# A gated long convolution with adapters: in the last stage's rounds, the projection ahead of the turn of the next gated tile

## The chip, the cores and the metric

The kernel runs on one core of a Trainium2 chip. The metric is device time of one execution in microseconds (us). Engines are TensorE (PE in the rows, PEld its weight loads), VectorE (DVE), ScalarE (ACT), GpSimd (POOL) and SyncE (SP, which issues most of the loads).

## What is computed

The input x is 8 sequences of 2048 rows with 512 channels, all float32. Two residual layers follow one another. The first is a Hyena layer, the second a weighted sum of 8 of 32 adapters, which is one 512 x 512 matrix and one bias for all rows.

```python
x = x + hyena(layernorm(x))
x = x + ffn(layernorm(x))

# hyena
proj = (x @ in_proj_w + in_proj_b).reshape(B, L, C, 3)
v = conv3(proj[..., 0]) + short_b
for i in range(2):
    conv = irfft(rfft(v) * rfft(coefs[:, :, i]))[:, :L]   # long convolution
    output = proj[..., i + 1] * conv
return output @ out_w + out_b

# ffn
return einsum('k,kod,bsd->bso', weights, W[ids], x) + einsum('k,ko->o', weights, b[ids])
```

Only the last branch reaches the output, so one long convolution and one gate are computed.

## The kernel before

The kernel has four parts: `prep` makes the filters' spectrum, `front` the normalised input, its two projections and the first transform, `middle` the product with the filter in the frequency domain, and `back` everything behind. The change is in `back`.

`back` works on 128 tiles of 128 rows and 512 channels, 16 for each of the 8 sequences. For each tile t:

- conv (L1361): the last step of the inverse transform, on TensorE, into the bank b_psC. Four matmul instructions with 64 columns of weights for each tile; `conv_pair` does two tiles in every second round.
- gate: GpSimd makes the correction at the sequence's edges (`correct`, L1294 and L1296, one product and one subtraction), VectorE adds it to b_psC (L1435) and multiplies with the gate from memory into b_o (L1440, the semaphore o_done).
- turn_o (L1375): four TensorE transposes of b_o into the bank b_psP, which is a single one (semaphore p_ps).
- o_high on ScalarE (L1312) copies b_psP, rounded to the matmul's type, into b_oh; o_low on VectorE (L1452) takes the rest into b_ol (o_lo). With it b_psP is free again.
- project: twelve matmuls of 512 columns (L181 to L183), high by high, high by low and low by high over four blocks of channels, into b_psO (o_ps).
- residual on VectorE: the sum with x (L1460, y_done), bn_stats (L1462), bn_aggr (L1468, mv_done). GpSimd makes scale and shift of it (`scalars`, L1276 to L1281, norm_ready) and then the sum of y and the second bias (`bias_y`, L1302). ScalarE's norm (L1318, z_done) writes the normalised tile b_z.
- turn_z (L1392), z_high (L1325), z_low (L1472): the same turn and split for b_z, through the bank b_psT.
- adapt: twelve matmuls into b_psF (L181 to L183, ff_ps). VectorE's finish (L1479) adds b_yb, and ScalarE's queue issues the store.

Each engine runs its own in-order program, and semaphores tie them together. The helper `pipelined` writes each engine's program: in round s it calls every stage in the list's order, with tile s minus the stage's lag. The same list stands for the first rounds (fill), the loop over the sequences and the last rounds (drain). The order inside a round is thus that of the list alone. VectorE's list is gates of tile s-1, residual s-3, z_low s-4, o_low s-1, finish s-5, bias_x s (L1429). ScalarE's is z_high s-4, o_high s-1, norm s-3, store s-6. GpSimd's is correct s, scalars s-3, bias_y s-3. SyncE loads the convolved rows (b_fin, waits for c_ps), the gate (b_gin, waits for o_done) and x (b_xin, waits for y_done).

On TensorE an odd round s does conv of tiles s-1 and s, turn_z of s-4, adapt of s-5, turn_o of s-1 and project of s-2. An even round does adapt of s-5, turn_z of s-4, turn_o of s-1 and project of s-2. The two forms of turn_z are why a pair of rounds repeats and not one.

Of the kernel before, what the change touches and what calls it, by code (L numbers as in the profile page):

```python
# [14 lines left out]
B = 8  # L15
# [6 lines left out]
T = 16  # L22
# [112 lines left out]
def pipelined(eng, outer, tiles, stages):  # L135

    fill = max(lag for _, lag in stages)

    def step(i, s, last):
        for stage, lag in stages:  # L140
            t = s - lag
            if t >= tiles and not last:
                stage(i + 1, t - tiles)
            elif 0 <= t < tiles:
                stage(i, t)

    for s in range(fill):
        step(0, s, False)

    def one_pass(i, last):  # L150
        for s in range(fill, tiles + fill):
            step(i, s, last)

    one_pass(0, False)
    with eng.Fori(1, outer - 1) as i:
        one_pass(i, False)
    one_pass(outer - 1, True)


def old(b, t, n):  # L160

    return not (isinstance(b, int) and b * T + t < n)


def hyena_adapter_kernel(nc, x, in_w, in_b, short_w, short_b, fw1, fb1, fw2, fb2, fw3, fb3,
# [13 lines left out]
    def mm3(pe, out_ps, w_hi, w_lo, d_hi, d_lo, first, last):  # L179

        pe.matmul(out_ps, w_hi, d_hi, start=first, stop=False)  # L181
        pe.matmul(out_ps, w_hi, d_lo, start=False, stop=False)  # L182
        return pe.matmul(out_ps, w_lo, d_hi, start=False, stop=last)  # L183
# [949 lines left out]
    def back(bc, kept):  # L1133
        with ExitStack() as st:
# [64 lines left out]
            def no(b, t):  # L1199
                return b * T + t  # L1200

            def early(b, t):
                return isinstance(b, int) and b == 0 and t < EARLY
# [7 lines left out]
            def turned_at(b, t):  # L1211
                if isinstance(b, int) and b == 0 and t in TURN_AT:
                    return range(2 * TURN_AT.index(t), 2 * TURN_AT.index(t) + 2)
                return ()
# [126 lines left out]
            @block.tensor  # L1341
            def _(pe):
                pe.wait_ge(kept["s4_in"], 16)
                pe.wait_ge(bc["ident_in"], 16)

                def turn_w(b, t):
                    for d in turned_at(b, t):
                        if d >= 2:
                            pe.wait_ge(wf_lo, d - 1)
                        for ot in range(CT):  # L1350
                            mm = pe.transpose(psF[d % 2][:, ot * P:(ot + 1) * P], res[:, ot, d * P:(d + 1) * P], ident[:])
                        mm.then_inc(wf_ps, 1)

                def conv(b, t):
                    pe.wait_ge(f_in[t % 2], 16 * (b * (T // 2) + t // 2 + 1))
                    if early(b, t):
                        pe.wait_ge(bc["tail_in"][t], 48)
                    if old(b, t, 2):
                        pe.wait_ge(a_done, no(b, t) - 1)
                    for h in range(2):  # L1360
                        mm = pe.matmul(psC[t % 2][h * N1:(h + 1) * N1, :], s4[:, h * T + t, :], fin[:, t % 2, h, :], start=True, stop=True)  # L1361
                    mm.then_inc(c_ps, 1)

                def conv_pair(b, t):

                    if t % 2:
                        conv(b, t - 1)
                        conv(b, t)

                def turn_o(b, t):  # L1370
                    pe.wait_ge(o_done, no(b, t) + 1)
                    if old(b, t, 1):
                        pe.wait_ge(o_lo, no(b, t))
                    for ct in range(CT):
                        mm = pe.transpose(psP[:, ct * P:(ct + 1) * P], o[:, t % 2, ct * P:(ct + 1) * P], ident[:])  # L1375
                    mm.then_inc(p_ps, 1)

                def project(b, t):
                    pe.wait_ge(o_lo, no(b, t) + 1)
                    if old(b, t, 2):  # L1380
                        pe.wait_ge(y_done, no(b, t) - 1)
                    for ct in range(CT):
                        mm = mm3(pe, psO[t % 2][:], oh[:, t % 2, ct * P:(ct + 1) * P], ol[:, t % 2, ct * P:(ct + 1) * P],
                                 woh[:, ct], wol[:, ct], ct == 0, ct == CT - 1)
                    mm.then_inc(o_ps, 1)

                def turn_z(b, t):
                    pe.wait_ge(z_done, no(b, t) + 1)
                    if old(b, t, 1):
                        pe.wait_ge(z_lo, no(b, t))  # L1390
                    for ct in range(CT):
                        mm = pe.transpose(psT[:, ct * P:(ct + 1) * P], z[:, t % 2, ct * P:(ct + 1) * P], ident[:])  # L1392
                    mm.then_inc(t_ps, 1)

                def turn_z_behind_conv(b, t):
                    if t % 2:
                        turn_z(b, t)

                def turn_z_behind_adapt(b, t):
                    if t % 2 == 0:
                        turn_z(b, t)

                def adapt(b, t):
                    pe.wait_ge(z_lo, no(b, t) + 1)
                    if isinstance(b, int) and b * T + t == 0:
                        pe.wait_ge(wf_lo, CT)
                    if old(b, t, 2):
                        pe.wait_ge(res_done, no(b, t) - 1)  # L1410
                    for ct in range(CT):
                        mm = mm3(pe, psF[t % 2][:], zh[:, t % 2, ct * P:(ct + 1) * P], zl[:, t % 2, ct * P:(ct + 1) * P],
                                 wfh[:, ct], wfl[:, ct], ct == 0, ct == CT - 1)
                    mm.then_inc(ff_ps, 1)

                pipelined(pe, B, T, [(conv_pair, 0), (turn_w, 0), (turn_z_behind_conv, 4), (adapt, 5), (turn_z_behind_adapt, 4), (turn_o, 1), (project, 2)])

            @block.vector
            def _(dve):
# [150 lines left out]
```

## Time and profile before

| | us |
|---|---|
| median of 3 runs | 2336.48 (2334.76 to 2341.91) |
| the profiled execution | 2337.87 |
| its span, first to last instruction | 2336.1 |
| TensorE busy | 2292.4, 98% |
| VectorE busy | 1530.6, 66% |
| GpSimd busy | 933.2, 40% |
| ScalarE busy | 855.8, 37% |

Busy time is a union over the whole span. The matmuls' ends are modelled and neighbours overlap, so distances are best taken from start to start. A bracket behind a timeline row says how long the engine was idle ahead of it and what released it. Bytes moved are 493.98 MB, at a mean of 211 GB/s.

### The profile page before, as it was taken

What the parts mean: (1) busy time and instruction counts of PE and PEld (TensorE: products, weight loads), DVE (VectorE), ACT (ScalarE), POOL (GpSimd) and SP (SyncE); (2) the same over time, 40 slices, a digit from 0 to 9 for tenths busy, and PEclk for the clock granted to TensorE, in tenths of its full rate; (3) what the DMA queues carried; (4) which work ended last, traced back from release to release, by engine and by line L of the source; (5) the groups of instructions that cost most, each with busy time, mean ns of one, the idle gap of its engine ahead of it and who ended that gap; (6) DMA issues with size and microseconds to landing.
All of it is one profiled execution on the core that took longest, in us unless ns stands there. A gap on an engine that the chain in (4) does not pass through costs nothing.

```text
span 2336.1 us, 39721 instructions
## 1 busy us (share of the span) xinstructions
PE 2292.4 (98%) x12804; PEld 1588.9 (68%) x12804; DVE 1530.6 (66%) x2180; ACT 855.8 (37%) x1155; POOL 933.2 (40%) x1183
## 2 busy tenths in 40 slices
PE   8899999999999999999999979999999999999999
PEld 2577777777777777543343337777777777777777
DVE  7644434444444434467777767888888888888886
ACT  5444444444444444344444432222222222222222
POOL 2222222222222222000000027777777777777775
PEclk9999999999999999999999989999999999999999
DMA  8645454545454456588999988765666666666663
GB/s 293 209 164 184 144 167 144 180 166 191 137 184 159 150 182 242 221 331 358 370 359 359 359 308 259 213 180 177 180 180 180 177 178 177 177 180 178 177 179 105
DMA packets 179725, 493.98 MB, mean 211 GB/s; under 512 B 19139, under 2 KB 19460, under 8 KB 158796
## 3 DMA queue, kind: packets, MB, share of 16 engines
q1 hardware_dynamic: 149964, 392.47, 51.2%
q10 hardware_dynamic: 29696, 100.68, 12.2%
q8 instruction: 35, 0.57, 0.1%
q14 instruction: 30, 0.25, 0.0%
HBM read 274.93 MB, written 218.12 MB: 211 GB/s over the span
## 4 chain that ended last, share of the span: by engine, by line
PE 54%; DMA 3%; SPq 0%; POOL 0%; issue 0%; DVE 0%; ACT 0%; DVEq 0%; POOLq 0%
PE m_psW L1046 8%; PE m_psA L1029 7%; PE b_psF L183 5%; PE b_psF L181 5%; PE b_psF L182 5%; PE b_psC L1361 5%; PE b_psO L181 5%; PE b_psO L183 5%; PE b_psO L182 5%; PE b_psT L1392 3%; PE b_psP L1375 2%; DMA m_xin<-spec 1%; DMA b_fin<-wide_out 0%; DMA b_fin<-spec 0%; DMA spec<-wide_out 0%
## 5 line engine op out<-in xcount | busy, mean ns | idle before, releaser
L1129 DVE TENSOR_TENSOR m_m<-m_psA,m_spec 128x1024 f32<-128x1024 f32 x256 | 301.3, 1219 | 103.9 <-PE m_psA L1029 86.3
L764 POOL TENSOR_TENSOR vl<-v,vh 128x512 fp32r<-128x512 f32 x128 | 165.2, 1291 | 389.7 <-ACT vh L722 389.7
L1046 PE MATMUL m_psW<-m_m,mats 64*64 64x512 f32 x2048 | 250.1, 592 | 2.0 <-issue 1.7
L1325 ACT ACTIVATE b_zh<-b_psT 128x512 fp32r<-128x512 f32 x128 | 76.5, 598 | 460.5 <-PE b_psT L1392 460.5
L865 DVE TENSOR_TENSOR gto<-psG,bgr 128x512 f32<-128x512 f32 x128 | 87.5, 683 | 195.2 <-PE psG L183 195.1
L181 PE MATMUL psV<-wvh,nth 128*128 128x512 f32 x512 | 213.3, 417 | 0.6 <-DVE ntl L846 0.6
L181 PE MATMUL b_psO<-woh,b_oh 128*128 128x512 f32 x512 | 211.2, 413 | 0.0
L1029 PE MATMUL m_psA<-m_xin,mats 64*64 64x512 f32 x1536 | 201.6, 598 | 6.4 <-PEq L555 3.0
L722 ACT ACTIVATE vh<-v 128x512 fp32r<-128x512 f32 x128 | 80.9, 632 | 340.6 <-DVE v L858 340.6
L181 PE MATMUL b_psF<-wfh,b_zh 128*128 128x512 f32 x512 | 205.4, 401 | 0.0
L182 PE MATMUL psV<-wvl,nth 128*128 128x512 f32 x512 | 200.6, 392 | 0.0
L183 PE MATMUL psV<-wvh,ntl 128*128 128x512 f32 x512 | 200.4, 391 | 0.0
L183 PE MATMUL b_psF<-wfh,b_zl 128*128 128x512 f32 x512 | 200.2, 391 | 0.0
L183 PE MATMUL b_psO<-woh,b_ol 128*128 128x512 f32 x512 | 200.1, 391 | 0.0
L182 PE MATMUL b_psO<-wol,b_oh 128*128 128x512 f32 x512 | 199.7, 390 | 0.0
L183 PE MATMUL psG<-wgh,ntl 128*128 128x512 f32 x512 | 199.5, 390 | 0.0
L181 PE MATMUL psG<-wgh,nth 128*128 128x512 f32 x512 | 199.2, 389 | 0.0
L182 PE MATMUL psG<-wgl,nth 128*128 128x512 f32 x512 | 199.2, 389 | 0.0
L182 PE MATMUL b_psF<-wfl,b_zh 128*128 128x512 f32 x512 | 199.1, 389 | 0.0
L846 DVE TENSOR_TENSOR ntl<-psT,nth 128x512 fp32r<-128x512 f32 x128 | 88.1, 688 | 168.4 <-ACT nth L716 168.4
L1085 ACT ACTIVATE wide_out<-m_psW 128x1024 f32<-128x1024 f32 x128 | 131.1, 1024 | 171.7 <-PE m_psW L1046 171.7
L1046 PEld LDWEIGHTS m_psW<-m_m,mats 64*64 64x64 f32 x2048 | 94.4, 133 | 129.7 <-issue 128.9
(138 smaller groups left out, 4652.4 us busy)
## 6 DMA issues: line engine op xcount, KB each, us to landing
spec<-wide_out SPq DMA_DIRECT2D x64, 1024.0 KB, 9.0
spec<-wide_out ACTq DMA_DIRECT2D x64, 1024.0 KB, 6.5
b_fin<-spec SPq DMA_DIRECT2D x126, 512.0 KB, 4.6
m_xin<-spec SPq DMA_DIRECT2D x30, 2048.0 KB, 10.0
xg<-in_L_attn_x_dram SPq DMA_DIRECT2D x64, 512.0 KB, 6.2
gate_d<-gto SPq DMA_DIRECT2D x32, 1024.0 KB, 4.0
b_gin<-gate_d SPq DMA_DIRECT2D x128, 256.0 KB, 3.6
b_xin<-in_L_attn_x_dram SPq DMA_DIRECT2D x256, 128.0 KB, 3.2
```

What stands on the lines that cost most here:

```text
L181: pe.matmul(out_ps, w_hi, d_hi, start=first, stop=False)
L182: pe.matmul(out_ps, w_hi, d_lo, start=False, stop=False)
L183: return pe.matmul(out_ps, w_lo, d_hi, start=False, stop=last)
L722: act.activation(vh[:, t % 2], v[:, t % 2], ACT.Copy).then_inc(v_hi, 1)
L764: pool.tensor_tensor(vl[:, t % 2], v[:, t % 2], vh[:, t % 2].bitcast(F32), ALU.subtract).then_inc(v_lo, 1)
L846: dve.tensor_tensor(ntl[:, t % 2], psT[t % 2][:].rearrange("p (k r) -> p k r", k=CT), nth[:, t % 2].bitcast(F32), ALU.subtract).then_inc(n ...
L865: dve.tensor_tensor(gto[:, slot, t % SUB], psG[:], bgr[:], ALU.add).then_inc(g_out, 1)
L1029: mm = pe.matmul(psA[k % RA][half[q], slot, :], w[half[slot]], xin[half[slot], par, B if k < 2 else 2 * (k - 2) + q, :], start=True, stop= ...
L1046: mm = pe.matmul(psW[pair % 2][half[slot], q, :], ws[slot][half[q]], m[half[q], pair % RM, part, slot, :], start=part == 0, stop=part == 1)
L1085: act.activation(wo[:, par, 2 * pair:2 * pair + 2, :], psW[pair % 2][:], ACT.Copy).then_inc(w_out, 1)
L1129: dve.tensor_tensor(m[:, (k - 2) % RM, part], psA[k % RA][:], spec[:, par, part], ALU.mult).then_inc(m_done, 1)
L1361: mm = pe.matmul(psC[t % 2][h * N1:(h + 1) * N1, :], s4[:, h * T + t, :], fin[:, t % 2, h, :], start=True, stop=True)
```

## The change

In TensorE's list of stages for `back`, `project` (lag 2) now stands ahead of `turn_o` (lag 1). A round thus ends with the turn of the tile gated in it, and the next round begins behind that. The instructions are the same in kind and number, each has the same waits and semaphores, and the other engines' programs are untouched.

```diff
--- before.py
+++ after.py
@@ -1413,7 +1413,7 @@
                                  wfh[:, ct], wfl[:, ct], ct == 0, ct == CT - 1)
                     mm.then_inc(ff_ps, 1)
 
-                pipelined(pe, B, T, [(conv_pair, 0), (turn_w, 0), (turn_z_behind_conv, 4), (adapt, 5), (turn_z_behind_adapt, 4), (turn_o, 1), (project, 2)])
+                pipelined(pe, B, T, [(conv_pair, 0), (turn_w, 0), (turn_z_behind_conv, 4), (adapt, 5), (turn_z_behind_adapt, 4), (project, 2), (turn_o, 1)])
 
             @block.vector
             def _(dve):
```

## Rows read from the trace of the kernel before

**Rows 1.** Busy time by stretch: from:to, length, each engine's busy us, clock, DMA.

```profile
1310.00:1410.00 100.00, 87.06 (x663) 41.80 (x656) 68.87 (x76) 37.34 (x43) 23.99 (x30) 0.93 0.87 318
1510.00:1610.00 100.00, 100.00 (x492) 74.99 (x490) 84.06 (x124) 26.49 (x41) 73.97 (x97) 1.00 0.62 180
```

**Rows 2.** Timeline of TensorE, one pair of rounds: start us, duration us, instruction.

```profile
1741.09 1.94 PE L1361 MATMUL b_psC<-b_fin,b_s 128*64 128x512 f32 x8
...
1742.95 0.66 PE L1392 MATMUL b_psT<-b_ident,b_z 128*128 128x128 f32 x4
...
1743.37 0.47 PE L181 MATMUL b_psF<-wfh,b_zh 128*128 128x512 f32 x1
...
1746.20 0.60 PE L1375 MATMUL b_psP<-b_ident,b_o 128*128 128x128 f32 x4
...
1746.55 0.47 PE L181 MATMUL b_psO<-woh,b_oh 128*128 128x512 f32 x1
...
1749.38 0.39 PE L181 MATMUL b_psF<-wfh,b_zh 128*128 128x512 f32 x1
...
1752.11 0.60 PE L1392 MATMUL b_psT<-b_ident,b_z 128*128 128x128 f32 x4
...
1752.54 0.60 PE L1375 MATMUL b_psP<-b_ident,b_o 128*128 128x128 f32 x4
...
1752.90 0.48 PE L181 MATMUL b_psO<-woh,b_oh 128*128 128x512 f32 x1
...
1755.81 1.94 PE L1361 MATMUL b_psC<-b_fin,b_s 128*64 128x512 f32 x8
```

**Rows 3.** Timeline of ScalarE, behind the first turn_o of rows 2.

```profile
1746.83 0.60 ACT L1312 ACTIVATE b_oh<-b_psP 128x512 fp32r<-128x512 f32 x1 [2.59 <-PE b_psP L1375]
```

**Rows 4.** Timeline of all engines, from one bn_aggr through o_low to the next.

```profile
1789.92 0.18 DVE L1468 BATCH_NORM_AGGREGATE b_mv<-b_stats 128x2 f32<-128x6 f32 x1 [0.18 <-DVE b_stats L1462]
...
1790.99 0.60 ACT L1312 ACTIVATE b_oh<-b_psP 128x512 fp32r<-128x512 f32 x1 [2.59 <-PE b_psP L1375]
...
1791.36 1.30 POOL L1302 TENSOR_TENSOR b_yb<-b_y,adb_sum 128x512 f32<-128x512 f32 x1
...
1791.62 0.69 DVE L1452 TENSOR_TENSOR b_ol<-b_psP,b_oh 128x512 fp32r<-128x512 f32 x1 [0.95 <-ACT b_oh L1312]
...
1792.63 1.28 POOL L1294 TENSOR_TENSOR b_corr<-b_edge_b,b_v 128x512 f32<-128x512 f32 x1
1792.83 1.63 DVE L1429 TENSOR_TENSOR b_xin<-b_xin,bor 128x512 f32<-128x512 f32 x1
...
1793.99 1.62 POOL L1296 TENSOR_TENSOR b_corr<-b_edge_b,b_corr 128x512 f32<-128x512 f32 x1
...
1797.67 0.18 DVE L1468 BATCH_NORM_AGGREGATE b_mv<-b_stats 128x2 f32<-128x6 f32 x1 [0.18 <-DVE b_stats L1462]
```

**Rows 5.** Timeline, bn_aggr and the norm that waited for it through GpSimd.

```profile
1782.09 0.18 DVE L1468 BATCH_NORM_AGGREGATE b_mv<-b_stats 128x2 f32<-128x6 f32 x1 [0.18 <-DVE b_stats L1462]
...
1783.61 0.82 ACT L1318 ACTIVATE b_z<-b_y,b_shift,b_rstd 128x512 f32<-128x512 f32 x1 [0.34 <-POOL b_shift L1281]
```

**Rows 6.** Timeline of the fill, norm and a turn_z that waited for it.

```profile
1403.02 0.81 ACT L1318 ACTIVATE b_z<-b_y,b_shift,b_rstd 128x512 f32<-128x512 f32 x1 [3.40 <-POOL b_shift L1281]
...
1403.89 0.66 PE L1392 MATMUL b_psT<-b_ident,b_z 128*128 128x128 f32 x4 [0.42 <-ACT b_z L1318]
```

**Rows 7.** Timeline of VectorE near the end, first and last of eight instructions.

```profile
2306.82 0.69 DVE L1452 TENSOR_TENSOR b_ol<-b_psP,b_oh 128x512 fp32r<-128x512 f32 x1 [1.47 <-ACT b_oh L1312]
...
2311.55 0.18 DVE L1468 BATCH_NORM_AGGREGATE b_mv<-b_stats 128x2 f32<-128x6 f32 x1 [0.18 <-DVE b_stats L1462]
```

**Rows 8.** Groups by line: busy us, mean ns of one | idle us before them.

```profile
L1429 DVE TENSOR_TENSOR b_xin<-b_xin,bor 128x512 f32<-128x512 f32 x128 | 145.8, 1139 | 7.4 <-DMA b_xin<-in_L_attn_x_dram 4.2 <-PEq L884 3.2
...
L1440 DVE TENSOR_TENSOR b_o<-b_corr,b_gin 128x512 f32<-128x512 f32 x128 | 141.4, 1105 | 13.3 <-DVE b_corr L1435 10.0
```

**Rows 9.** DMA issues on the page: count, KB each, median us to landing.

```profile
b_fin<-spec SPq DMA_DIRECT2D x126, 512.0 KB, 4.6
```

## Prediction

> **What bounds the kernel now.** I read the page's slices first, then stretches of the last stage. From 1.41 ms to the end TensorE is at 100% with the full clock, while VectorE stands at 84%, GpSimd at 74% and ScalarE at 26% [rows 1]. The last stage is a repeating pair of rounds: an odd round A (conv_pair, turn_z, adapt, turn_o, project) and an even round B (adapt, turn_z, turn_o, project). TensorE's timeline gives it without a hole: A from 1741.09 to 1749.38, B to 1755.81, a pair of 14.72 us, 7.36 a tile [rows 2]. Starting with round 5 there are 61 such periods. So time can only come from shorter work on TensorE or go into waits that TensorE doesn't have now. VectorE is next: its own queue has little over one microsecond to spare in a round, and it is chained to TensorE through ScalarE.
>
> **What is moved on TensorE.** Nothing is added or taken away: four transposes of turn_o(s-1) go behind the twelve matmuls of project(s-2). Its waits go with it: turn_o waits for o_done(s-1) and o_lo(s-2), project for o_lo(s-2) and y_done(s-4). All four are met earlier today than either needs them, so project can move up at no cost.
>
> Junctions first. An adapt or project behind its own kind takes 2.73 us (B's adapt), behind a transpose 2.83 (A's adapt and project), and 2.91 where the conv follows it; a turn takes 0.35 to 0.36 ahead of a project, 0.43 where another turn follows, and 0.42 behind the conv; the conv takes 1.86 [rows 2]. After the change A is 1.86 + 0.42 + 2.83 + 2.73 + 0.35 = 8.19, and B is 2.83 + 0.35 + 2.83 + turn_o. A turn followed by the conv isn't in the trace; its bounds are 0.35 and 0.43, and I take 0.40, as a change of kind of work cost 0.08 on the other side. B is 6.41, the pair 14.60. Without any wait the change would save 0.12 a pair, 61 x 0.12 = 7.3 us.
>
> **What the move delays.** turn_o now starts 2.7 us later in its round, and everything that hangs on it does too: o_high on ScalarE, o_low on VectorE. Behind o_low in VectorE's queue stand finish, bias_x, and the next round's gate (two operations), residual (add, bn_stats, bn_aggr) and z_low. Behind o_high in ScalarE's queue stands norm. TensorE doesn't need o_low soon, there is an adapt between. But it needs norm, and norm needs bn_aggr, which stands in VectorE's queue behind the o_low of the round before. That closes a loop through all engines. From the turn_o that ends round A:
>
> - turn_o to o_high: 1746.20 to 1746.83, 0.63 [rows 2, 3]
> - o_high to o_low: 1790.99 to 1791.62, 0.63 [rows 4]
> - o_low to the bn_aggr of round B: X, eight VectorE instructions, below
> - bn_aggr through four small GpSimd steps to norm: 1782.09 to 1783.61, 1.52 [rows 5]
> - norm to turn_z, where TensorE did wait for it once: 1403.02 to 1403.89, 0.87 [rows 6]
> - turn_z of the next round A 0.42, adapt 2.83, project 2.73, and then turn_o again [rows 2]
>
> The loop is 9.63 + X and runs once in a pair. If it is over 14.60, that is X over 4.97, TensorE waits at turn_z of round A; against today's 14.72 the change loses from X = 5.09 on. Today turn_o of A stands ahead of project, so the same loop is 2.73 shorter, 6.90 + X, and never binds.
>
> **The size of X.** Undisturbed it is 4.73 (2306.82 to 2311.55, near the kernel's end) [rows 7]. Two of the eight read two SBUF operands, bias_x and the gate's product; undisturbed they take about 0.68, but on average 1.139 and 1.105 [rows 8], so 0.46 + 0.42 more, which gives X = 5.61. One of the longest is 1791.62 to 1797.67, 6.05 [rows 4]. The same rows show why: bias_x issued at 1792.83 ends 0.55 after the GpSimd product of 1792.63 (1.28 long), so it waited for that instruction to end, and the GpSimd subtraction issued at 1793.99 took 1.62 in place of 1.28, behind bias_x. Either engine waits out the other's instruction.
>
> The Trainium skill says so too (SBUF — State Buffer, "SBUF: two separate sides"): VectorE with two SBUF inputs and GpSimd take their shared ports by an exclusive lock, and the loser blocks for the whole instruction. By these rows the trace agrees. A reader who takes the lock for a mere sharing would use the mean of 5.61; one who goes by the rule has to ask which instruction meets which, and the next paragraph does so from rows.
>
> After bn_aggr of round A GpSimd starts bias_y 1.44 later, the product 2.71 and the subtraction 4.07 later, the last until about 5.35 [rows 4]. In the new steady state o_low of A starts 9.63 - Y after that same bn_aggr, Y being VectorE's way from B's bn_aggr to A's: 4.73 and one z_low (some 0.7) and its own waits of about 0.9 to 1.0, so 6.4. Then o_low stands at 3.2 and bias_x, 1.21 behind it [rows 4], at 4.4: inside the subtraction, till 5.35 + 0.55. It takes some 1.4 in place of 0.6, and the gate's product then meets no GpSimd work. That gives X = 5.55. Both ways agree; I take 5.6. Bounds: 4.73 and 6.05.
>
> **Sum.** Pair: 9.63 + 5.6 = 15.23, against 14.72: +0.51, of which TensorE's wait is 0.63 and the junctions give 0.12 back. 61 x 0.51 = 31 us. The profiled execution has a time of 2337.9 (span 2336.1), 1.4 over the median of 2336.5; 2337.9 + 31 = 2369. The fill and the last rounds have other bounds and I cost them at nothing: the fill waits for transfers, and in the drain the last project stands behind an adapt either way.
>
> **What else is moved past, at no cost.** TensorE issues no DMAs. SP's loads follow c_ps, o_done and y_done. The gate's product and residual come up to 2.7 us later in the round; the load of the convolved rows behind them takes 4.6 us to land [rows 9] and is needed at the next conv_pair, a pair of over 14 us later. If that cover were gone, a conv would be late by what is missing, but some 4 us are left. finish comes later too, and the adapt that reuses its bank is a round away. z_low of A should end over 1 us ahead of B's adapt, and the gate's product of B 0.8 us ahead of the turn_o that ends B.
>
> **Rivals.** (1) **The loop doesn't bind, and the kernel is not slower.** For it: VectorE is idle for over 1 us in many rounds, and X of 4.73 exists. It decides at X below 5.09: bias_x would have to be issued after the GpSimd subtraction's end or ahead of its start (0.3 us from where I put it). At 4.73 the pair is 14.60: 2337.9 - 7.3 = 2331; with a short wait, X = 5.1, it is 2338. Against it: the mean X of 5.61, and only an undisturbed stretch is so short. (2) **More meetings.** If bias_x and the gate's product both meet GpSimd's work, X = 6.05, the pair 15.68, +0.96 x 61 = 59: 2396. Then VectorE's A stretch lengthens as well and z_low of A may become late for adapt, with about 1 us of cover. (3) **The clock.** Where TensorE was busy only 87% of a stretch its granted clock was 0.93 on average, against 1.00 at 100% [rows 1]. The waits here leave it 96% busy. If it nonetheless came to 0.93, TensorE's own share of the loop (0.63, 0.42, 2.83 and 2.73, together 6.6) would grow by 0.5 and the pair to 15.73, just over the 14.6 us of work, which grow to 15.7: 61 x 0.5 = 30 us more, 2400 in all. The Trainium skill (TensorE: Matmul & The Clock Gate, "A second HAM failure mode: psum-queue depth-cycling") tells of short idle times between groups of matmuls that make the clock oscillate; that rule gives this rival, and rows of the last stage, having no waits, can't show it. (4) **It does not do what it says**, that is, the order stays: the four transposes are issued in program order, and I give it nothing.
>
> **How the numbers follow.** The loop with X between 5.2 and 5.95, so 2344 to 2391: 0.72. Rival 1 with its short waits, up to 2344: 0.14, of which 0.03 ends below 2329.5, since its best case of 2331 gets there only if the junctions cost less than I took, and 0.11 is within. Rival 2: 0.09. Rival 3: 0.05. The range from 2340 (X at 5.1, a little of rival 1) to 2396 (X at its upper bound) should hold 8 in 10. About 0.3%, 7 us, is what a measurement of this kernel can tell from no change: faster 0.03, same 0.11, slower 0.86.
>
> **What the profile will show.** Right: TensorE idle some 0.6 us before b_psT in every second round, released by ScalarE's b_z, some 40 us in all; VectorE idle 2 to 2.5 us before b_ol in round A; pairs of 15.2 us; ScalarE's wait for b_psP longer. A pair of 14.60 would mean that X is short or that norm comes by another way. A wait of TensorE before b_psF for VectorE's b_zl, or before b_psP for b_o, would show a loop that I hold to be slack. A granted clock below 0.99 in the last stage would be rival 3. The prediction is wrong if VectorE's idle time before b_ol doesn't appear, or if bias_x no longer meets GpSimd.

## The result and the profile after

| | before | after |
|---|---|---|
| median, us | 2336.7 | 2366.53 |
| ratio to before | | 1.0129, 95% interval 1.0115 to 1.0143 |
| span of the profiled execution, us | 2336.1 | 2365.7 |
| a pair of rounds, us | 14.72 | 15.24 |

The changed kernel is 1.3% slower, 30 us. The prediction said 2369, in a range of 2340 to 2396.

One stretch by engine (from:to, length, busy us of TensorE, its weight loads, VectorE, ScalarE and GpSimd, the granted clock, the share and rate of the DMAs). It answers to the second row of [rows 1]:

```profile
1510.00:1610.00 100.00, 97.53 (x474) 73.49 (x474) 78.25 (x117) 25.36 (x39) 68.72 (x92) 1.00 0.60 174
```

TensorE has 2.5 us of idle time in 100, where it had none. Everybody else is less busy too: no engine has become the bound, a wait has. The clock is as before.

Who waits for whom from 1500 to 2200 us, in the changed kernel (total us, times, longest us):

```profile
ACT b_oh L1312 <- PE b_psP L1375: 365.2, 92, 5.4
...
DVE b_ol L1452 <- ACT b_oh L1312: 109.1, 45, 2.6
...
PE b_psT L1392 <- ACT b_z L1318: 18.5, 46, 0.5
```

The third row is the loss: TensorE waits ahead of turn_z for the normalised tile, 46 times, once in each pair, 0.40 us each. The second is what it comes from: VectorE waits 2.4 us for o_high, once in each pair.

The loop in the changed kernel's timeline, from the turn_o that ends a round A:

```profile
1787.87 0.60 PE L1375 MATMUL b_psP<-b_ident,b_o 128*128 128x128 f32 x4
...
1788.58 0.60 ACT L1312 ACTIVATE b_oh<-b_psP 128x512 fp32r<-128x512 f32 x1 [5.39 <-PE b_psP L1375]
...
1789.22 0.69 DVE L1452 TENSOR_TENSOR b_ol<-b_psP,b_oh 128x512 fp32r<-128x512 f32 x1 [2.54 <-ACT b_oh L1312]
...
1789.97 1.29 POOL L1296 TENSOR_TENSOR b_corr<-b_edge_b,b_corr 128x512 f32<-128x512 f32 x1
1790.42 1.39 DVE L1429 TENSOR_TENSOR b_xin<-b_xin,bor 128x512 f32<-128x512 f32 x1
...
1794.27 0.60 PE L1375 MATMUL b_psP<-b_ident,b_o 128*128 128x128 f32 x4
...
1794.65 0.18 DVE L1468 BATCH_NORM_AGGREGATE b_mv<-b_stats 128x2 f32<-128x6 f32 x1 [0.18 <-DVE b_stats L1462]
...
1794.80 1.94 PE L1361 MATMUL b_psC<-b_fin,b_s 128*64 128x512 f32 x8
...
1796.17 0.81 ACT L1318 ACTIVATE b_z<-b_y,b_shift,b_rstd 128x512 f32<-128x512 f32 x1 [0.67 <-POOL b_shift L1281]
...
1797.04 0.66 PE L1392 MATMUL b_psT<-b_ident,b_z 128*128 128x128 f32 x4 [0.31 <-ACT b_z L1318]
```

Follow it step by step: turn_o 1787.87, o_high 1788.58, o_low 1789.22, bn_aggr 1794.65, norm 1796.17, turn_z 1797.04. No link has spare time in it, and norm waits for the last of GpSimd's small steps (0.67 us in its bracket), not for its place behind o_high. X, from o_low to bn_aggr, is 5.43 in this pair, one of the shortest; over the 45 whole pairs from 1500 to 2200 us its mean is 5.58. In the kernel before X is as long, 5.62 on the mean of 47 pairs (6.05 in [rows 4]), but there norm lies 3.04 us ahead of its turn_z on the mean; here it is 0.87, the distance of a turn_z that waited for its norm [rows 6]. So it is not VectorE's stretch that has grown, but the rest of the loop, by the project that now stands in it. Two more things stand in the rows. bias_x meets GpSimd's subtraction and takes 1.39; and the turn_o at 1794.27 holds the conv until 1794.80, 0.53 later.

The two operations with two SBUF inputs over the whole stage, which answer to [rows 8]:

```profile
L1429 DVE TENSOR_TENSOR b_xin<-b_xin,bor 128x512 f32<-128x512 f32 x128 | 172.3, 1346 | 3.2 <-PEq L884 3.2
...
L1440 DVE TENSOR_TENSOR b_o<-b_corr,b_gin 128x512 f32<-128x512 f32 x128 | 105.8, 827 | 13.3 <-DVE b_corr L1435 10.0
```

bias_x has gone from 1.139 to 1.346 us and the gate's product from 1.105 to 0.827. These are means over both kinds of round. Inside X alone, from 1500 to 2200 us, bias_x has gone from 1.19 to 1.52 and the product from 1.06 to 0.69, as the two now stand in other places against GpSimd's work. What the second gains pays for what the first loses.

### The profile page after: what moved, and what is told of

It is laid out like the page before. It is cut to its first block, busy times and chain, and to the rows that moved or that the text cites. A ratio compares the mean times of both kernels' runs of the same rounds, so it can differ in the third digit from the quotient of the medians.

```text
span 2365.7 us, 39721 instructions
## 1 busy us (share of the span) xinstructions
PE 2296.7 (97%) x12804; PEld 1592.5 (67%) x12804; DVE 1517.9 (64%) x2180; ACT 858.8 (36%) x1155; POOL 916.6 (39%) x1183
## 4 chain that ended last, share of the span: by engine, by line
PE 25%; POOL 14%; issue 13%; DVE 3%; DMA 2%; ACT 1%; POOLq 0%; SPq 0%; DVEq 0%; ACTq 0%
PE m_psW L1046 9%; PE m_psA L1029 7%; POOL b_corr L1294 5%; POOL b_corr L1296 5%; POOL b_rstd L1279 2%; PE b_psF L181 1%; PE b_psF L183 1%; PE b_psF L182 1%; PE b_psO L183 1%; PE b_psO L181 1%; PE b_psO L182 1%; DVE b_xin L1429 1%; ACT b_z L1318 1%; PE b_psT L1392 1%; POOL b_rstd L1276 1%
## 5 line engine op out<-in xcount | busy, mean ns | idle before, releaser
L1312 ACT ACTIVATE b_oh<-b_psP 128x512 fp32r<-128x512 f32 x128 | 76.5, 598 | 517.9 <-PE b_psP L1375 517.9
L181 PE MATMUL b_psF<-wfh,b_zh 128*128 128x512 f32 x512 | 212.1, 414 | 0.0
L181 PE MATMUL b_psO<-woh,b_oh 128*128 128x512 f32 x512 | 205.6, 401 | 1.4 <-DVE b_ol L1452 1.4
L1452 DVE TENSOR_TENSOR b_ol<-b_psP,b_oh 128x512 fp32r<-128x512 f32 x128 | 88.4, 691 | 160.2 <-ACT b_oh L1312 156.6
```

What stands on the lines that cost most here:

```text
L1452: dve.tensor_tensor(ol[:, t % 2], psP[:], oh[:, t % 2].bitcast(F32), ALU.subtract).then_inc(o_lo, 1)
```

## The experiments

Where a run changes the kernel after, the diff is against that; "TensorE's list" is that of `back`. The theory is the loop of the prediction. The expectations name three rivals by letters: A, the cost is TensorE's own, in switches between kinds of matmul; B, norm is late because it stands behind o_high in ScalarE's queue; C, VectorE's own work makes X long and GpSimd has no part in it.

### bias_x out of the loop

```diff
-pipelined(dve, B, T, [(gates, 1), (residual, 3), (z_low, 4), (o_low, 1), (finish, 5), (bias_x, 0), (w_low, 0)])
+pipelined(dve, B, T, [(gates, 1), (residual, 3), (z_low, 4), (bias_x, 0), (o_low, 1), (finish, 5), (w_low, 0)])
```

> The changed kernel with one stage moved on VectorE: bias_x ahead of o_low, not behind finish. It then lies outside the eight instructions from o_low to bn_aggr. The loop theory: X falls by bias_x's 1.4 us to about 4.2, the loop to 14.0, under TensorE's own work of a pair. The turn followed by the conv takes 0.53 us in the changed kernel's trace, so this work is 14.73 and not 14.60: no wait of TensorE, a pair of 14.73, 2337 us, no difference from the kernel before. Rival A, the cost is TensorE's own (switches between kinds of matmul): 2366, as VectorE's order changes nothing. Rival B, norm is late because it stands behind o_high in ScalarE's queue: 2366.

Measured: 2341.5, a ratio of 1.0023 (1.0013 to 1.0033). The loss is gone but for 5 us. The same stretch of this kernel:

```profile
1510.00:1610.00 100.00, 100.00 (x490) 74.72 (x489) 71.26 (x122) 26.62 (x42) 75.19 (x94) 1.00 0.65 176
```

TensorE is full again. Its timeline, with VectorE's and one GpSimd step:

```profile
1748.06 0.69 DVE L1452 TENSOR_TENSOR b_ol<-b_psP,b_oh 128x512 fp32r<-128x512 f32 x1 [2.67 <-ACT b_oh L1312]
...
1752.18 0.18 DVE L1468 BATCH_NORM_AGGREGATE b_mv<-b_stats 128x2 f32<-128x6 f32 x1 [0.18 <-DVE b_stats L1462]
...
1752.85 0.68 DVE L1429 TENSOR_TENSOR b_xin<-b_xin,bor 128x512 f32<-128x512 f32 x1
1752.85 1.09 POOL L1279 TENSOR_TENSOR b_rstd<-b_rstd,b_power 128x1 f32<-128x1 f32 x1
...
1753.20 0.60 PE L1375 MATMUL b_psP<-b_ident,b_o 128*128 128x128 f32 x4
...
1753.72 1.94 PE L1361 MATMUL b_psC<-b_fin,b_s 128*64 128x512 f32 x8
```

VectorE still waits 2.67 us for o_high, so turn_o is as late as in the changed kernel, and it costs nothing: X is 1748.06 to 1752.18, 4.12. TensorE's order, its instructions and the switches between them are those of the changed kernel. That rules out rival A for the most part; its remainder is this kernel's pair, 14.79 over the stage against 14.72, and 61 x 0.07 = 4 us is what is left of the loss.

The control is the same move of bias_x in the kernel before.

> The control of the run above: the same move of bias_x in the kernel before. All theories: TensorE is busy without a hole, a pair of 14.72, 2336 us, within 2 us of the kernel before. If it were faster, the move would be worth something of its own and the run above would not test the loop.

Measured: 2337.9, ratio 1.0014 (1.0003 to 1.0024), a pair of 14.72. The move gains nothing by itself.

### project ahead in one kind of round alone

```diff
+def turn_o_odd(b, t):
+    if t % 2 == 0:
+        turn_o(b, t)
+
+def turn_o_even(b, t):
+    if t % 2:
+        turn_o(b, t)
...
 odd rounds alone, in the list of before:
-(turn_o, 1), (project, 2)])
+(turn_o_even, 1), (project, 2), (turn_o_odd, 1)])
 even rounds alone:
-(turn_o, 1), (project, 2)])
+(turn_o_odd, 1), (project, 2), (turn_o_even, 1)])
```

> The kernel before with project ahead of turn_o in odd rounds (A) alone. The loop theory: turn_o of A is as late as in the changed kernel, so o_low, bias_x, the gate and so on of round B are late too, while turn_o of B now stands ahead of project and wants the gate's product 2.8 us sooner. From turn_o of A: 0.7 + 0.63 to o_low, 3.3 to the product, 0.9 to its end and on to turn_o of B, then 0.35, 2.91, 1.86, 0.42, 2.83, 2.73 to the next turn_o of A: 15.7 to 16.6. That is worse than the changed kernel, 2395 to 2420 us, with TensorE waiting at b_psP for b_o in round B. Rival A (switches): half of the change's cost or less, 2337 to 2352. Rival B (norm behind o_high): about 2366 or less.

Measured: 2400.7, ratio 1.0279 (1.0262 to 1.0296), a pair of 15.74. Half of the change costs twice the whole. The timeline of a round B in this kernel:

```profile
1739.82 0.69 DVE L1460 TENSOR_TENSOR b_ol<-b_psP,b_oh 128x512 fp32r<-128x512 f32 x1 [3.75 <-ACT b_oh L1312]
...
1742.34 0.69 DVE L1448 TENSOR_TENSOR b_o<-b_corr,b_gin 128x512 f32<-128x512 f32 x1
...
1743.09 0.65 PE L1375 MATMUL b_psP<-b_ident,b_o 128*128 128x128 f32 x4 [0.75 <-DVE b_o L1448]
```

TensorE waits for the gate's product, which stands behind the same late o_low, once in each pair. From turn_o of A to turn_o of B it is 4.57 on the mean, and TensorE's own work from there to the next turn_o of A is 11.18; together they are the whole pair. norm's loop has room here: X is 4.74, as bias_x and the product meet nothing (0.68 and 0.69), and norm lies 2.23 ahead of turn_z. It is another branch of the same tree: everything behind o_low in VectorE's queue is late, and what TensorE asks for first decides. In the changed kernel turn_o of B has been moved back too, so this branch has time and norm's is the first.

> The kernel before with project ahead of turn_o in even rounds (B) alone. The loop theory: turn_o of A is early as before, and turn_o of B, 2.8 us later, has a chain of 0.7 + 0.63 + 5.6 + 1.5 + 0.9 = 9.3 us to turn_z of the next B, which starts 11.0 us behind it. No wait: TensorE's own work, 14.73 a pair, 2337 us. Rival A: as for the odd rounds, the turn of 0.53 ahead of the conv stands here, so half the cost or all of it, 2350 to 2366. Rival B: o_high of B holds norm, which turn_z of A needs soonest, so nearly all of the cost, 2360 to 2366.

Measured: 2345.0, ratio 1.0039 (1.0023 to 1.0056), a pair of 14.82. The even half is almost free. The loop theory put it at 2337, which is too low; 14.79 of the pair is TensorE's own work with the slow switch ahead of the conv, and the rest is some short waits, here from 1500 to 2200 us:

```profile
PEld b_psP L1375 <- DVE b_o L1448: 7.4, 23, 0.4
```

The eight runs lie in two groups, 2340 to 2342 and 2348 to 2350; the profile is of the lower, and what the upper group adds isn't known. Rival A would have had half of the cost or more here, where the slow switch is, 2350 to 2366. Rival B would have had nearly all of it.

### The meeting with GpSimd

```diff
-pool.tensor_tensor(corr[:, t % 2], edge(0, t), v0b, ALU.mult).then_inc(corr_step, 1)
-pool.wait_ge(corr_step, no(b, t) + 1)
 pool.tensor_tensor(corr[:, t % 2], edge(1, t), corr[:, t % 2], ALU.subtract).then_inc(corr_done, 1)
```

> The changed kernel without GpSimd's product of the edge correction (L1294); the subtraction stays and starts where the product did, 2.7 us behind bn_aggr, and ends at 4.0. The output lacks that product. VectorE's and TensorE's instructions are the same. The loop theory with X made long by meetings: bias_x, about 4.4 us behind bn_aggr, meets no GpSimd work, X falls from 5.5 to about 4.75, the loop to 14.4, under TensorE's own 14.79: a pair of 14.79, 2341 us. Rival C, X is long by VectorE's own work and GpSimd's use doesn't matter: 2366.

Measured: 2341.5, ratio 1.0026 (1.0013 to 1.0039), a pair of 14.78. VectorE's and TensorE's programs are those of the changed kernel; the output lacks the product. The timeline:

```profile
1747.66 0.69 DVE L1450 TENSOR_TENSOR b_ol<-b_psP,b_oh 128x512 fp32r<-128x512 f32 x1 [1.58 <-ACT b_oh L1310]
1748.11 1.30 POOL L1294 TENSOR_TENSOR b_corr<-b_edge_b,b_corr 128x512 f32<-128x512 f32 x1
...
1748.87 1.08 DVE L1427 TENSOR_TENSOR b_xin<-b_xin,bor 128x512 f32<-128x512 f32 x1
...
1752.79 0.18 DVE L1466 BATCH_NORM_AGGREGATE b_mv<-b_stats 128x2 f32<-128x6 f32 x1 [0.18 <-DVE b_stats L1460]
```

In this pair bias_x still meets the end of the subtraction, but that makes it only 0.4 us longer (it ends 0.54 behind it), and X is 5.13, the longest there is. Over the 47 pairs from 1500 to 2200 us X lies between 4.72 and 5.13, with a mean of 4.86: on the mean well under the point at which the wait begins, 5.13 (see the junctions, below). Inside X bias_x takes 0.80 on the mean, where it took 1.52, and that is all of the 0.72 by which X is shorter; the gate's product takes 0.69 in both. So the wait for GpSimd inside bias_x is needed for the loss, against rival C. The loss doesn't belong to the order of TensorE's list alone: on the mean 0.7 us less in VectorE's stretch takes the whole wait away.

### norm ahead of o_high on ScalarE

```diff
-pipelined(act, B, T, [(z_high, 4), (o_high, 1), (norm, 3), (w_high, 0), (store, 6)])
+pipelined(act, B, T, [(z_high, 4), (norm, 3), (o_high, 1), (w_high, 0), (store, 6)])
```

> The changed kernel with norm ahead of o_high in ScalarE's list. Rival B (norm is late because it stands behind o_high): norm no longer waits for the late turn_o, the wait of TensorE at turn_z goes, about 2341. The loop theory: norm is late because bn_aggr is; with norm ahead, o_high waits for norm, and a loop closes in every round and not in every pair: norm to o_high 0.5 to 0.8, 0.63 to o_low, X of 5.4 to 5.6, 1.52 to the next norm, 8.1 to 8.6 a round, 16.2 to 17.2 a pair: 2425 to 2490, much slower.

Measured: 2448.7, ratio 1.0483 (1.0447 to 1.0520), a pair of 16.68. The timeline:

```profile
1747.17 0.81 ACT L1318 ACTIVATE b_z<-b_y,b_shift,b_rstd 128x512 f32<-128x512 f32 x1 [4.57 <-POOL b_shift L1281]
1747.89 0.58 ACT L1312 ACTIVATE b_oh<-b_psP 128x512 fp32r<-128x512 f32 x1
...
1748.50 0.69 DVE L1452 TENSOR_TENSOR b_ol<-b_psP,b_oh 128x512 fp32r<-128x512 f32 x1 [2.10 <-ACT b_oh L1312]
...
1754.53 0.18 DVE L1468 BATCH_NORM_AGGREGATE b_mv<-b_stats 128x2 f32<-128x6 f32 x1 [0.18 <-DVE b_stats L1462]
...
1756.06 0.82 ACT L1318 ACTIVATE b_z<-b_y,b_shift,b_rstd 128x512 f32<-128x512 f32 x1 [6.73 <-POOL b_shift L1281]
```

From norm to norm: 0.72, 0.61, 6.03, 1.53, together 8.89. This is the longer of the two rounds of its pair; the mean round is 8.34. TensorE has dropped out of this loop, which is why it runs once in a round. norm is late because its input is, and rival B is wrong: where it was taken at its word, the kernel lost 82 us more. By itself this run could be read as the cost of a new loop alone; the changed kernel's own row of norm, with its 0.67 us of waiting for GpSimd's last step after o_high had ended, says the same of rival B without it.

### A longer link

```diff
+pool.tensor_tensor(spare[:], eps[:], power[:], ALU.pow).then_inc(spare_set, 1)
+pool.wait_ge(spare_set, no(b, t) + 1)
 pool.tensor_tensor(r, mv[:, 1:2], eps[:], ALU.add).then_inc(pow_step, 1)
```

The tile `spare` and its semaphore are new and serve nothing else. The control has the same step in the kernel before.

> The changed kernel with one more small GpSimd step (a power of 128 x 1 into a spare tile, and a wait for it) in each tile's way from bn_aggr to norm; such a step takes 0.63 us from start to start. The loop theory: the way is run through once in a pair and nothing hides it, so a pair grows from 15.23 by 0.6 to about 15.85, and the time by some 38 us to 2404; 2390 to 2410, as meetings of VectorE and GpSimd may move a little. Rival A (TensorE's switches): 2366, GpSimd has 30% idle time.

> The same step added to the kernel before, as control. There the loop is 6.9 + X, some 12.5 us, and 2 us of slack in a pair are left: a pair of 14.72, 2336 us within 3. If it were slower too, the run above would only show that GpSimd's work costs time anywhere.

Measured: in the changed kernel 2390.0, ratio 1.0235 (1.0218 to 1.0252), which is 23 us over the changed kernel, not 38; in the kernel before 2337.2, ratio 1.0010 (1.0000 to 1.0019). The same instruction costs over 20 us in one order and under 5 in the other. The size was missed, and the timeline of the longer kernel shows where it went:

```profile
1783.16 0.69 DVE L1456 TENSOR_TENSOR b_ol<-b_psP,b_oh 128x512 fp32r<-128x512 f32 x1 [2.42 <-ACT b_oh L1316]
1783.31 1.30 POOL L1298 TENSOR_TENSOR b_corr<-b_edge_b,b_v 128x512 f32<-128x512 f32 x1
...
1784.37 0.79 DVE L1433 TENSOR_TENSOR b_xin<-b_xin,bor 128x512 f32<-128x512 f32 x1
1784.69 1.62 POOL L1300 TENSOR_TENSOR b_corr<-b_edge_b,b_corr 128x512 f32<-128x512 f32 x1
...
1785.88 0.97 DVE L1444 TENSOR_TENSOR b_o<-b_corr,b_gin 128x512 f32<-128x512 f32 x1
...
1788.37 0.18 DVE L1472 BATCH_NORM_AGGREGATE b_mv<-b_stats 128x2 f32<-128x6 f32 x1 [0.18 <-DVE b_stats L1466]
```

The step has moved GpSimd's work back against VectorE's. bias_x now comes in ahead of the subtraction, takes 0.79 in place of 1.39, and it is the subtraction that waits (1.62). But the late subtraction now meets the gate's product, which takes 0.97 where it took 0.69. Over the stretch from 1500 to 2200 us bias_x in X is 0.72 shorter on the mean (0.80) and the product 0.36 longer (1.05). X is 5.21 here. Link by link, as means from start to start over the pairs from 1500 to 2200 us:

| | turn_o to o_high | to o_low | X | to norm | to turn_z | to turn_o | sum |
|---|---|---|---|---|---|---|---|
| predicted | 0.63 | 0.63 | 5.60 | 1.52 | 0.87 | 5.98 | 15.23 |
| after | 0.65 | 0.63 | 5.58 | 1.53 | 0.88 | 5.97 | 15.24 |
| longer link | 0.65 | 0.63 | 5.21 | 2.16 | 0.88 | 5.98 | 15.51 |
| bias_x ahead | 0.65 | 0.63 | 4.14 | 2.13 | 1.26 | 5.98 | 14.79 |
| product left out | 0.65 | 0.63 | 4.86 | 1.54 | 1.12 | 5.98 | 14.78 |

The added 0.63 is all there, and X gave 0.37 back. The pair is thus 0.27 longer, and 61 x 0.27 is 16.5 of the 23 us. By the starts of the conv the 61 periods take 17.8 us more than in the changed kernel's trace, of 21.4 between the two spans; 1.1 lies ahead of them and 2.5 behind, in the last rounds. In the last two rows the way from norm to turn_z is over 0.88: that is spare time in the loop, and TensorE's own work sets the pair. Where bias_x stands ahead, norm is 0.6 later behind its bn_aggr, because bias_x now meets one of GpSimd's small steps (L1279 takes 1.09 in the rows above, 0.55 in the changed kernel), and the loop has 0.4 left nonetheless.

## Why the prediction was right

**The bound.** TensorE without a hole, and so only a loss through a new wait or a gain in switches: right. No kernel's median went below that of the kernel before.

**The loop.** Right in its links and in its sum, 15.23 against 15.24. The two ways to X, the mean of the long instructions (5.61) and the placing of bias_x inside the subtraction (5.55), both hit the measured 5.58. The second is the one that the runs bear out. By its placing, from 4.4 to 5.35 + 0.55, bias_x takes 1.5 (the words "some 1.4 in place of 0.6" are loose: undisturbed it takes 0.68), and in X it takes 1.52 on the mean, 1.38 to 1.64. The gate's product met nothing (0.69 in every pair), and where the meeting was moved or removed, X moved with it. The mean came out right by luck, as it was made of two waits and the changed kernel has one longer and one shorter.

**The junctions.** This step failed. A turn ahead of the conv was bounded by 0.35 and 0.43, from turns ahead of other work [rows 2], and put at 0.40; it takes 0.53. An adapt or a project behind a turn is 2.84 to 2.86 and not 2.83, three times in a pair. Together that is the missing 0.19. TensorE's own pair is 14.79, not 14.60, so the order saves nothing, it costs 0.07. The total did not suffer, since the slow turn ends round B and lies beside the loop, not in it: the pair is the larger of the two, 15.24 in either case. But the parts are another: of the 0.52 a pair has lost, 0.45 is the wait (15.24 against 14.79) and 0.07 the switches, where the prediction had 0.63 and a gain of 0.12. The point where the wait begins lies at X = 14.79 - 9.66 = 5.13, not 4.97. And rival 1, at its best, ends at about 2341 and not at 2331, which two runs show (bias_x ahead, and the product left out, both 2341.5): the few per cent for a faster kernel had nothing under them.

**The signs in the profile.** VectorE's wait before b_ol was told as 2 to 2.5 us and is 2.4. TensorE's wait before b_psT in every second round is there, released by b_z; its total was told as 40 us and is 61 x 0.45 = 27 (0.40 each in the wait's own row, where the end of the matmul ahead of it is modelled). The waits of TensorE for b_zl and b_o, held to have room, are absent in the changed kernel, and the second appears as soon as turn_o of B stands early and that of A late. The clock of the profiled execution is 0.995 (0.994 before). Rival 3, the clock, was built on a misread mean; the last section has the rows.

**What stayed open.** Why the switch from a turn to the conv takes 0.53 wasn't tried apart; the one place where it stands was in every kernel with an early project in even rounds, and it was the same in all.

## What to carry to other kernels

An order in one engine's program is bought from slack in all others. Before moving a step back, follow what it releases through every in-order queue until the chain comes back to the same engine, add up the links from start to start, and compare the sum with the engine's own work in that period. A chain that is far from binding in one place may bind one step later, and the half of a change can be worse than the whole, when it makes a result late but leaves early the step that needs it. The length of a link that shares a resource with another engine isn't a constant: place it in time rather than take its mean.

## What was not expected of the hardware

A group of four transposes ahead of the 64-column conv takes 0.53 us to the next start, against 0.35 ahead of a matmul of 512 columns and 0.43 ahead of another turn. The other way round, the turn behind the conv takes 0.41 in all kernels, 0.06 more than a turn between two groups of 512-column matmuls (0.35).

TensorE's granted clock stayed at 1.00, the level of 2.4 GHz, in stretches where it was busy 97.5% of the time with a hole of about 0.4 us in each 15, in the changed kernel. With norm ahead of o_high it was busy 90% only, with waits of up to 1.2 us, and the clock was the same:

```profile
1510.00:1610.00 100.00, 90.27 (x433) 66.61 (x432) 70.60 (x108) 22.77 (x36) 62.04 (x84) 1.00 0.55 158
```

So rival 3, the clock, which the prediction took from a stretch of 87% with 0.93 [rows 1] and from the Trainium skill (TensorE: Matmul & The Clock Gate, "A second HAM failure mode: psum-queue depth-cycling"), was not at work at this spacing. Nor is the 0.93 a level of the clock. It is the mean of a stretch that ran at 1.00 but for two parts at 0.50, the level of 1.2 GHz, both in the first rounds of `back`, where the conv waited for a load. In the kernel before:

```profile
1310.00:1368.00 58.00, 57.78 (x536) 22.98 (x528) 45.30 (x39) 27.95 (x28) 5.07 (x4) 1.00 0.93 362
1372.00:1378.00 6.00, 2.56 (x6) 0.80 (x8) 0.48 (x1) 0.00 (x0) 0.00 (x0) 0.50 0.54 223
1389.00:1395.00 6.00, 4.96 (x18) 3.26 (x19) 4.74 (x7) 0.20 (x1) 3.33 (x3) 0.50 1.04 328
...
1375.44 3.39 PE L1361 MATMUL b_psC<-b_fin,b_s 128*64 128x512 f32 x8 [6.93 <-DMA b_fin<-wide_out]
...
1390.04 1.98 PE L1361 MATMUL b_psC<-b_fin,b_s 128*64 128x512 f32 x4 [3.86 <-DMA b_fin<-spec]
```

Each fall came inside one of the two waits, of 6.93 and 3.86 us, and the clock was back by 1379 and 1396 us. So the sum of 2400 for rival 3 spread over all pairs what belonged to two long waits ahead of them. Shorter ones can come before a fall too: in the last rounds, behind the pairs, the clock fell to 0.50 just behind a wait of 2.0 us with the longer link and of 2.5 us with norm ahead, while the changed kernel's 1.39 and 1.50 there left it at 1.00. The longest wait from 1500 to 2200 us in any run is 1.2 us.
